# A fused transformer kernel on one core: the variance as two products of rounded parts, and another order of work on GpSimd

## What is computed

```python
def attn_layer(x, Wqkv, qs, ksc, Wo):
    q, k, v = jnp.split(x @ Wqkv, 3, -1)          # then heads
    q = l2norm(q) * qs;  k = l2norm(k) * ksc      # rotary tables, scaled
    out = local_attention(q, k, v)                # windows of 32, softmax
    return out.transpose(0, 2, 1, 3).reshape(b, n, INNER) @ Wo

def ffn_layer(x, g, bln, W1, b1, W2, b2):
    mu = x.mean(-1, keepdims=True)
    var = ((x - mu) ** 2).mean(-1, keepdims=True)
    xn = (x - mu) / jnp.sqrt(var + 1e-05) * g + bln
    a, gate = jnp.split(xn @ W1 + b1, 2, -1)
    return a * jax.nn.gelu(gate, approximate=False) @ W2 + b2

for i in range(6):
    x = attn_layer(shift_tokens(x), Wqkv[i], ...) + x
    x = ffn_layer(shift_tokens(x), ln_g[i], ...) + x
```

## Time and profile before

| | |
|---|---|
| median of 3 runs | 1634.13 us (1633.86 to 1638.28) |
| the profiled execution | 1644.43 us, of which 1642.6 are the span of the trace |
| mean granted TensorE clock | 0.973 |
| PE busy | 1557.8 us, 95% of the span, x37082 |
| DVE busy | 1304.4 us, 79% |
| ACT busy | 1295.9 us, 79% |
| POOL busy | 1235.2 us, 75% |

### The profile page before, as it was taken

One profiled execution on the slowest core, in us unless ns is written; L12 is line 12 of the kernel. 1 busy time (PEld: TensorE's weight loads), 2 busy tenths in 40 slices (PEclk: granted clock), 3 DMA queues, 4 the chain that ended last, 5 costly groups with the idle time before them and its releaser, 6 DMA issues.

```text
span 1642.6 us, 90368 instructions
## 1 busy us (share of the span) xinstructions
PE 1557.8 (95%) x37082; PEld 1276.5 (78%) x37082; DVE 1304.4 (79%) x1945; ACT 1295.9 (79%) x2058; POOL 1235.2 (75%) x954
## 2 busy tenths in 40 slices
PE   7898689999999999999999999999999999999977
PEld 3575578887888887888888888887888878888866
DVE  5475868888888887888888888888888888888853
ACT  5596557888788888888888888888788888888863
POOL 2201758889888889889889788889888888888831
PEclk9798799999999999999999999999999999999988
DMA  3000224332334223324233243332343223322221
GB/s 129 2 0 1 50 53 112 75 71 53 88 76 121 70 53 72 93 68 113 62 73 72 77 111 75 75 72 52 93 117 75 67 53 75 93 69 68 62 65 39
DMA packets 75873, 116.75 MB, mean 71 GB/s; under 512 B 17310, under 2 KB 27292, under 8 KB 74908
## 3 DMA queue, kind: packets, MB, share of 16 engines
q1 hardware_dynamic: 75804, 115.99, 28.3%
HBM read 19.04 MB, written 1.05 MB: 12 GB/s over the span
## 4 chain that ended last, share of the span: by engine, by line
PE 86%; issue 6%; POOL 4%; DVE 1%; ACT 1%; DMA 0%; POOLq 0%; SPq 0%; ACTq 0%; DVEq 0%
PE ps L702 16%; PE ps L968 9%; PE ps L943 9%; PE ps L894 9%; PE ps L819 8%; PE ps L822 7%; PE ps L823 7%; PE ps L887 3%; PE ps L990 3%; PE ps L691 2%; PE ps L992 2%; PE ps L991 2%; POOL arena L476 2%; POOL arena L467 1%; PE ps L979 1%
## 5 line engine op out<-in xcount | busy, mean ns | idle before, releaser
L467 POOL TENSOR_TENSOR arena<-arena 128x1024 f32<-128x1024 f32 x192 | 457.6, 2383 | 46.3 <-DVE arena L1667 32.5
L476 POOL TENSOR_TENSOR arena<-arena,rnorm 128x1024 f32<-128x1024 f32 x192 | 362.0, 1907 | 84.8 <-ACT rnorm L1265 84.1
L702 PE MATMUL ps<-cst,arena 64*128 64x64 f32 x6656 | 291.6, 231 | 29.3 <-issue 7.9
L702 PEld LDWEIGHTS ps<-cst,arena 64*128 64x128 f32 x6656 | 249.6, 141 | 88.1 <-issue 74.9
L1254 ACT ACTIVATE arena<-ps 128x1024 f32<-128x1024 f32 x192 | 197.0, 1026 | 105.5 <-DVE arena L1667 101.7
L1663 DVE TENSOR_TENSOR arena<-ps,rope 128x1024 f32<-128x1024 f32 x192 | 233.8, 1218 | 19.7 <-PE ps L823 18.0
L1667 DVE TENSOR_TENSOR arena<-ps,rope 128x1024 f32<-128x1024 f32 x192 | 233.2, 1215 | 0.0
L822 PE MATMUL ps<-wqkv_lo,x_hi 128*128 128x512 f32 x576 | 229.2, 398 | 0.0
L823 PE MATMUL ps<-wqkv_hi,x_hi 128*128 128x512 f32 x576 | 228.5, 397 | 0.0
L1677 DVE TENSOR_REDUCE norm<-arena 128x16 f32<-128x1024 f32 x192 | 224.5, 1209 | 0.3 <-ACT arena L1254 0.2
L819 PE MATMUL ps<-wqkv_hi,x_lo 128*128 128x512 f32 x576 | 200.9, 430 | 0.8 <-issue 0.6
(11 more groups left out here) (162 smaller groups left out, 3001.9 us busy)
## 6 DMA issues: line engine op xcount, KB each, us to landing
v_sb<-v_nat SPq DMA_DIRECT2D x576, 130.0 KB
v_sb<-v_nat SPq DMA_DIRECT2D x192, 65.0 KB
wqkv_sb<-wqkv SPq DMA_DIRECT2D x6, 1536.0 KB, 6.5
v_sb<-v_sb SPq DMA_DIRECT2D x96, 65.0 KB
wo_sb<-wo SPq DMA_DIRECT2D x6, 512.0 KB, 3.6
w_sb<-w SPq DMA_DIRECT2D x6, 341.0 KB
x<-xT SPq DMA_DIRECT2D x1, 1024.0 KB, 5.4
scl<-scales SPq DMA_DIRECT2D x6, 128.0 KB, 6.2
```

Source lines behind the costliest of these rows:

```text
L467: pool.tensor_tensor(t_cos[:, m, j, :], t_cos[:, m, j, :], t_sin[:, j, :], ALU.add)\
L476: pool.tensor_tensor(x, x, rnorm[:, H * j:H * j + H].unsqueeze(2).to_broadcast([P, H, D]), ALU.mult).then_inc(s[done], 1)
L702: mm = pe.transpose(ps[0:width, bank + t, 64 * c:64 * c + 64], src[r], ident[r, r], tile_position=(64 * t, 0))
```

## The change

Three parts, in one diff. TensorE's variance is made by `mean_of_parts`, like the mean, from the rounded square and its rest. GpSimd makes both parts in the new `part_square`, into the same tiles `f_nh` and `f_nl` that held the parts of x. Therefore the writers of x's parts now wait for the variance before and not for the mean. ScalarE's `square` moves ahead of `copy_q`. And GpSimd's order changes in slots with `after == 7`: x's rest comes before the scaling of the second half and before the table, V's weights are split behind the values' parts, and of the scaling of the next slot's first half only Q stays in its place, K comes after the norm's division and scaling. In the other slots only `part_square` is new, and `part_x` stays behind the scaling.

```diff
-            def scale(pair, m):
+            def scale(pair, m, which=(0, 1)):
                 n = 2 * pair + m
                 pool.wait_ge(s["inverted"], CREDIT + n + 1)
-                for j, done in ((0, "q_scaled"), (1, "k_scaled")):
+                for j in which:
+                    done = ("q_scaled", "k_scaled")[j]
...
             def part_x(f):
                 pool.wait_ge(s["f_x_rounded"], CREDIT + f + 1)
-                pool.wait_ge(s["f_mean"], CREDIT + f)
+                pool.wait_ge(s["f_var"], CREDIT + f)
...
+            def part_square(f):
+                pool.wait_ge(s["f_squared"], CREDIT + f + 1)
+                pool.wait_ge(s["f_mean"], CREDIT + f + 1)
+                pool.sem_inc(s["pool_waited"], 1)
+                pool.tensor_copy(f_nh[:, :], f_sq).then_inc(s["f_sq_rounded"], 1)
+                pool.wait_ge(s["f_sq_rounded"], CREDIT + f + 1)
+                pool.tensor_tensor(f_nl[:, :], f_sq, f_nh[:, :].bitcast(F32), ALU.subtract)\
+                    .then_inc(s["f_sq_parted"], 1)
...
                 f = g - 2
+                if norm and after == 7:
+                    part_x(f)
+                scale(g, 1)
+                if norm and after != 7:
+                    part_x(f)
                 if after == 7:
                     table(layer, 1)
-                scale(g, 1)
-                if norm:
-                    part_x(f)
                 if ahead:
                     rotate(g + 1, 0, 0)
                     low(g + 1, 1)
                     rotate(g + 1, 0, 1)
+                    if norm:
+                        part_square(f)
+                    if ff:
+                        part_gated(g - LAG)
                     if after == 7:
                         split_weights(layer, 2)
-                    if ff:
-                        part_gated(g - LAG)
                     if after == 3:
                         split_down(layer)
-                    scale(g + 1, 0)
+                    scale(g + 1, 0, (0,) if after == 7 else (0, 1))
...
                 if norm:
                     divide(f)
                     scale_norm(f)
+                if after == 7:
+                    scale(g + 1, 0, (1,))
...
                     if norm:
                         pe.wait_ge(s["centred"], CREDIT + 4 * g + 4)
-                        variance(g - 2, 2)
+                        mean_of_parts("f_sq_parted", g - 2, 2, "f_var")
...
             def round_x(f):
                 act.wait_ge(s["f_shifted"], CREDIT + 2 * f + 2)
-                act.wait_ge(s["f_mean"], CREDIT + f)
+                act.wait_ge(s["f_var"], CREDIT + f)
...
                 if ahead:
                     high(g + 1, 1)
                     square_of(g + 1, 0, 1)
+                if norm:
+                    square(g - 2)
                 if after == 7:
                     round_weights(layer, 2)
                 copy_q(g, 1)
...
                 if ff:
                     act.preload_act_table_set("natural_log_exp_and_others")

-                if norm:
-                    square(g - 2)
                 if att:
                     copy_o(g - 1, 1)
```

More of the change, by code:

```diff
@@ L245, in build @@
         f_shifted f_mean f_centred f_squared f_var f_log f_rstd f_normed f_scaled
-        f_high f_split w1_high w1_ready f_rounded f_parted w2_high w2_ready f_x_rounded f_x_parted
+        f_high f_split w1_high w1_ready f_rounded f_parted w2_high w2_ready f_x_rounded f_x_parted f_sq_rounded f_sq_parted
         f_gate_up f_value_up f_gated f_prod f_down f_done
```

## The result

| | before | after |
|---|---|---|
| median, us | 1638.17 (15 runs, in turn with those of after) | 1632.15 (15 runs, 1628.19 to 1640.56) |
| ratio after / before | | 0.9969, 95% interval 0.9954 to 0.9984 |
| profiled execution, us (span) | 1644.4 (1642.6) | 1637.57 (1635.6) |
| ordinary slot, median of 31, us (the means differ by 0.07) | 29.31 | 29.25 |
| boundary slot and the slot behind it, together, us | 60.56 to 60.62 in four, 61.37 in one | 60.22 to 60.31 |

What follows compares the result with a forecast made beforehand. TensorE, busy 86%, was taken to bound the kernel. Cheaper variances (46 x 0.19 = 8.7 us) and five boundaries (0.5) sum to 9.2 us off the 1634.1 median: 1624.9 us, range 1617 to 1631.

Steps and rivals of the forecast that it cites:

- The variance's price: TensorE's variance: one fp32 product of 0.43 us becomes two rounded products of 0.24 together, saving 0.19 us a slot.
- That it would be passed on: TensorE, slots 1 to 46: the 0.19 us shortens every slot, since no wait eats it; 8.7 us in all.
- ScalarE's square fits: ScalarE ahead of `copy_q`: the moved square fits in 0.51 us of idle, leaves 0.1 to 0.2 and costs nothing.
- The square brings no table load: ScalarE: the square runs with the Gelu set loaded; the rival, another table, gave some 1740 us, chance 0.01.
- GpSimd's two instructions: GpSimd, each slot: a cast and a subtraction take 1.15 us, cost nothing and leave 0.3 idle before Q's scaling.
- The boundary: Slot 7, layers 1 to 5: a 1.64 us wait traded for 0.8, 0.15 and 0.7; 0.5 us gained in all.
- What would be late next: V's products waiting for the variance's logarithm, or ScalarE's squares before it; both have some 0.2 to 0.4 us left.
- The saving isn't passed on: Rival: a loop through ScalarE and VectorE keeps slots at 29.3 us; 1634 us, chance 0.10.
- The boundary is won outright: Rival: the boundary's new waits don't arise, so each boundary's 1.97 us goes too; 1615.5 us, chance 0.12.
- the square doesn't fit: Rival: ScalarE's square misses the gap ahead of `copy_q` and delays `copy_k` and the mask products; 1649 us, chance 0.07.

Runs made afterwards that it cites:

- e1: The kernel before, with two unused semaphores that VectorE raises at its start; 1644.87 us, ratio 1.0048.
- e2: The changed kernel, with the two new semaphores raised at the start by SyncE instead of VectorE; 1633.17 us, ratio 0.9964.
- e7: The changed kernel, with one new semaphore raised by SyncE and the other by VectorE; a single run, 1638.7 us.
- e12: e11 with four more semaphore instructions at VectorE's start, on a semaphore nobody reads; 1627.2 us, ratio 0.9929.
- e6: The kernel before with GpSimd's new boundary order, and ScalarE's rounding of V's weights moved behind `copy_p`; 1628.26 us, ratio 0.9943.
- e10: e2 with ScalarE's rounding of V's weights behind `copy_p` and VectorE's loop written by layer; a single run, 1632.65 us.
- e9: e10 with V's split at the boundary on VectorE, behind its last rotary product, instead of GpSimd; 1642.6 us, ratio 1.0032.
- e4: The changed kernel with GpSimd's old order in slots 7, 15, 23, 31 and 39; 1637.14 us, ratio 0.9999.
- e11: e9 with VectorE's split of V's weights one step earlier, between the rotary products of the second half; 1628.62 us, ratio 0.9949.

## Why the prediction was right or wrong

**The variance's price was right.** 0.43 became 0.23, with no idle before the pair. The operands did lie ready.

**That it would be passed on was the step that failed.** The prediction says that TensorE's few waits run "without the variance between them, so a shorter variance isn't eaten by them". That sentence is true, and still the slot gained 0.07 instead of 0.19. It took TensorE's waits from the table as they were, and asked only whether the shorter variance would lengthen one. The wait of `turn_q(g, 1)` for VectorE's subtraction wasn't in the table, for it was worth under a tenth. It had no slack either: the subtraction's end and the transposes lie the same 0.26 apart in both kernels. Every delay of the subtraction was a delay of the slot, and an edit at VectorE's start brought one of 0.11. The prediction has no term for VectorE at all, so it put these two instructions at nothing without a reason. Over 46 slots that is 5.1 of the 8.7 us. e1 shows that the two added instructions alone do this, e2 that without them the slot is 29.14, 0.17 less than before. The last 0.02 aren't accounted for. That the delay was there to be met was luck of the place: with one instruction more instead of two (e7) the forecast for the ordinary slot, 29.12, would nearly have come true (29.15).

**ScalarE's square fits.** In the timeline of ScalarE in an ordinary slot of after, 0.18 of idle is left ahead of `copy_q`, where 0.1 to 0.2 was forecast and 0.51 stood before:

```profile
962.10 0.42 ACT L1348 ACTIVATE f_sq<-f_a 128x256 f32<-128x256 f32 x1
962.70 1.03 ACT L1289 ACTIVATE arena<-ps 128x1024 f32<-128x1024 f32 x1 [0.18 <-PE ps L718]
```

The square brings no table load: the two lines that load a table in the loops do so 45 times each, as before. The first of the two in after, by the groups of ScalarE:

```profile
L1406 ACT ACT_TABLE_LOAD x45 | 57.7, 1283 | 0.8
```

**GpSimd's two instructions** take 1.15 us as forecast, from 964.52 to 965.67. The idle left before Q's scaling is 0.73 here, more than the 0.3 forecast, since this is another slot than that of the earlier trace rows: slot 26 of before has not 1.47 but 1.76, and the inverse norm that the scaling waits for came 0.13 later. In the slots that had 1.5 before, about 0.46 is left, and in the slot behind a boundary nothing. Slot 26, after and then before:

```profile
964.52 0.39 POOL L528 CAST f_nh<-f_sq 128x256 fp32r<-128x256 f32 x1
964.99 0.73 POOL L530 TENSOR_TENSOR f_nl<-f_sq,f_nh 128x256 fp32r<-128x256 f32 x1
...
969.13 3.77 POOL L477 TENSOR_TENSOR arena<-arena,rnorm 128x1024 f32<-128x1024 f32 x2 [0.73 <-ACT rnorm L1282]
```

```profile
973.50 3.77 POOL L476 TENSOR_TENSOR arena<-arena,rnorm 128x1024 f32<-128x1024 f32 x2 [1.76 <-ACT rnorm L1265]
```

**The boundary came out nearly as worked out.** TensorE in slots 31 and 32 of after:

```profile
1094.25 0.71 PE L718 MATMUL ps<-cst,arena 64*128 64x64 f32 x16 [0.24 <-issue]
...
1112.38 0.30 PE L903 MATMUL ps<-mask_bf,ident_bf 64*64 64x256 bf16 x4 [0.85 <-ACT k_t L1298]
...
1121.13 0.73 PE L835 MATMUL ps<-wqkv_hi,x_lo 128*128 128x512 f32 x2
...
1126.44 0.71 PE L718 MATMUL ps<-cst,arena 64*128 64x64 f32 x16 [0.67 <-POOL arena L477]
```

The mask products wait 0.85 (0.8 was forecast), K 0.67 (0.7), V's products not visibly (0.15). A fourth wait, 0.24 before Q's transposes at the start of slot 31, wasn't on the list. The pair of slots 31 and 32 went from 60.57 to 60.23, -0.34, where two cheaper variances and 0.1 make -0.48; the two stops of VectorE, 0.22, explain the difference and more. In slot 23 the gain is 1.05, for a reason of its own (the clock, below).

**"What would be late next" came true in four slots.** In slots 11, 19, 27 and 35, where ScalarE jumps back in its loop over the layers, between its exponentials and its squares of the next Q and K, TensorE comes to V's products late, up to 0.25 us of it as a wait for the logarithm of the variance. Slot 19, TensorE, ScalarE and VectorE:

```profile
766.98 0.72 PE L835 MATMUL ps<-wqkv_hi,x_lo 128*128 128x512 f32 x2 [0.25 <-ACT f_a L1354]
```

```profile
765.55 1.03 ACT L1271 ACTIVATE arena<-ps 128x1024 f32<-128x1024 f32 x1 [2.52 <-DVE arena L1684]
```

```profile
763.41 1.21 DVE L1684 TENSOR_TENSOR arena<-ps,rope 128x1024 f32<-128x1024 f32 x1
```

ScalarE's square of Q stands ahead of the logarithm. The row puts its wait down to VectorE's product, but that had ended at 764.62, 0.93 us before; in the other slots the square follows the product by 0.12. The rest is ScalarE's own, at its jump: in these four slots of after the square follows by 0.7 to 0.9 us, in those of before by 0.6 to 1.0. The stretches that begin in them take 29.51 to 29.76, where before they took 29.29 to 29.73: on average they got 0.13 longer. The prediction had the wait and its 0.2 to 0.4 of room from an ordinary slot, and didn't look at the slots that are longer than the ordinary one. How long the jump takes changes from slot to slot also between kernels that don't touch ScalarE, so part of the 0.13 may be chance.

**The sum over slots 2 to 46**, 1330.0 to 1325.9, -4.1: 31 ordinary slots by 0.07, -2.2; five pairs, -2.4, of which 0.8 is slot 23's clock; four stretches with ScalarE's jump, +0.5. The forecast had -9.1 for the same stretch. Of the 5.0 missing, VectorE's stop has 45 x 0.11 = 5.0, and the +0.8 that the stretches with the jump lost against ordinary ones is paid by slot 23's 0.8. The kernel without the stop, e2, got back 3.4 of the 5.0 in its trace.

**The rivals.** "The saving isn't passed on" was nearest (it gave 1634) but for another reason than the one it named: not a loop through ScalarE and VectorE, but a stop in VectorE's stream. "The boundary is won outright" and "the square doesn't fit" didn't come. The lowest ratio of all, e12's, is 11.6 us (0.0071 x 1638, interval 7.7 to 15.4), by keeping the parts and taking V's split off GpSimd. But e6, the new order without any parts of the square, has 9.3 us (6.1 to 12.8), and the two can't be told apart.

## What to carry to other kernels

Besides the waits that a table shows, list those that show no idle but start a fixed distance behind another engine's end; they have no slack, and a tenth there is a tenth a slot. When a diff that shouldn't touch an engine makes a place on it later by a constant tenth in every pass, count the instructions that the diff put ahead in that engine's stream, and try the same kernel with a few more or with these on another engine. And when a reordering trades one long wait for several short ones, find the queue whose last event ends the stretch: moving work on another queue only moves the waits about (60.16 and 60.16), taking work off that one shortens it (59.22).

## What the runs showed of the hardware

**A stop at a place in the code.** VectorE's stream has a stop of about 0.105 us, seen when it runs on after a wait, whose place among its instructions moves when others are added far ahead (e1, e2, e7, e12) and which isn't found near the subtraction in some copies of the same code (e10). There the subtraction is 0.47 behind the product, in the other copies 0.59. It decides up to 5 us of this kernel (45 x 0.11). Its cause is open.

**A jump back costs by its place too.** VectorE's gap at the end of its loop is 0.29 us with one loop, 0.41 and 0.20 in two copies of the same body, and 0.75 at the outer loop (e10 to e12). ScalarE's first operation behind the jump of its loop over layers follows what it waited for by 0.6 to 1.0 us in before and after, elsewhere by 0.12, and this changes from pass to pass.

**The clock fell behind some long waits.** The views of three stretches of 5 us show, after the length, the busy time of PE, PEld, DVE, ACT and POOL with their instructions, then the granted clock. Before, right behind the wait of 1.6 us in slots 23 and 31, with the same part of the slot in both:

```profile
876.10:881.10 5.00, 4.89 (x178) 4.41 (x178) 4.17 (x7) 2.97 (x3) 4.76 (x4) 0.68 0.00 0
1113.40:1118.40 5.00, 4.88 (x244) 4.26 (x246) 4.20 (x7) 3.71 (x4) 4.76 (x4) 1.00 0.00 0
```

e9, behind the wait of 1.91:

```profile
1129.00:1134.00 5.00, 4.90 (x25) 3.92 (x27) 0.79 (x2) 1.95 (x4) 5.00 (x4) 0.66 0.00 0
```

0.68 and 0.66 are means of two values: shorter views of before give 1.00 from 875.0 to 877.8, 0.50 from 878.0 to 881.2 and 1.00 from 881.4 to 884.0, and those of e9 0.50 from 1130.6 to 1133.8. In before the engine is as busy, and gets 178 instructions done where it gets 244 in slot 31. The lower clock costs 0.8 us in slot 23 and 1.4 to 1.5 in e9. It followed one of five such waits of 1.5 to 2.0 us in before, two of five in e1 and in e4, three of five in e9, and none in after, where no wait of a boundary reaches 1 us. So 0.8 of the 1.05 us that slot 23 and the one behind it gained in after is the clock that wasn't lost; when it falls and when not, these runs don't say. In the rest of slots 2 to 46 the granted clock is 1.00 in all 14 traces; ahead of them its mean is 0.86 to 0.90, and behind them 0.84 to 1.00, so much of what whole runs scatter by need not lie in the slots.

**Beside VectorE's split GpSimd took longer.** In e9 GpSimd's `scale_norm` took 1.18 while VectorE's split ran, where it took 0.56 before. The split itself took 1.61 there and takes 1.29 in e11; no run has it without work of GpSimd beside it. In e11 GpSimd's scaling beside the split took 2.89, where it takes 1.90, in all five boundaries alike:

```profile
1110.94 1.29 DVE L1760 TENSOR_TENSOR wqkv_lo<-wqkv_sb,wqkv_hi 128x1024 fp32r<-128x1024 f32 x1
```

```profile
1111.10 2.89 POOL L479 TENSOR_TENSOR arena<-arena,rnorm 128x1024 f32<-128x1024 f32 x1
```

Both were seen beside this one operation of VectorE, whose two operands lie in SBUF. VectorE's rotary products, which read one of theirs from PSUM, run beside GpSimd in every slot, and there the scaling takes 1.90. Not all that GpSimd did beside the split took longer: in e9 the norm's division, more than half of it beside the split, took 0.72 to 0.73, against 0.75 before. Why the two operations took longer, no run shows. The price was 0.6 us a boundary in e9 and 1.0 in e11, so taking V's split off GpSimd gave back that much of the 2.36 us it freed.
